# A routed recurrent layer on one core: the slot table emptied group by group, six tiles of ids fetched directly, and five row buffers instead of six

## What is computed

```python
xn = layernorm(x)                              # 4 x 2048 tokens of 512 values
h[t] = h[t-1] * A + xn[t]; s = h @ BC           # recurrence over 8 runs of 1024 tokens
e = argmax(xn @ gate_w.T)                       # one of 8 experts for each token
g = silu(xn + expert_w[e] @ xn)
out = x + s * g
```

## Time and profile before

| | |
|---|---|
| median of 3 runs | 524.4 us (523.9 to 524.87) |
| the profiled execution | 521.92 us |
| its span, first to last instruction | 520.2 us |
| PE busy | 495.5 us, 95% of the span |
| VectorE busy | 409.0 us, 79% |
| ScalarE busy | 260.2 us, 50% |
| POOL busy | 325.1 us, 62% |
| mean granted clock of TensorE | 0.987 |

### The profile page before, as it was taken

How to read it: one execution, slowest core, us unless ns; L and a number is a source line. 1 busy time by engine, 2 the same in 40 slices (tenths; PEclk the granted TensorE clock), 3 DMA queues, 4 the chain that set the end, 5 groups by cost and what they waited for, 6 DMA issues and landing times. The chain is left out here.

```text
span 520.2 us, 10723 instructions
## 1 busy us (share of the span) xinstructions
PE 495.5 (95%) x2739; PEld 389.0 (75%) x2740; DVE 409.0 (79%) x1075; ACT 260.2 (50%) x500; POOL 325.1 (62%) x362
## 2 busy tenths in 40 slices
PE   7959999999999999999996999999999999999993
PEld 6647777777777777777675788888888888887882
DVE  5968998999999998899752777777778777776773
ACT  4647678667767766776621333333333333333330
POOL 3446766676676667667765466666676666656652
PEclk9979999999999999999999999999999999999997
DMA  8996878787788878777336676777767776766620
GB/s 243 394 342 178 258 241 247 233 269 227 253 258 234 249 237 263 228 243 234 120 97 193 224 226 222 234 239 244 249 213 234 235 243 214 232 221 212 222 82 9
DMA packets 65538, 116.99 MB, mean 225 GB/s; under 512 B 8906, under 2 KB 26378, under 8 KB 65428
## 3 DMA queue, kind: packets, MB, share of 16 engines
q1 hardware_dynamic: 47328, 64.59, 39.3%
q0 software_dynamic: 18176, 52.06, 31.6%
HBM read 66.30 MB, written 57.48 MB: 238 GB/s over the span
## 5 line engine op out<-in xcount | busy, mean ns | idle before, releaser
L1073 PE MATMUL ps_s<-w_hi,split 128*128 x284 | 118.2, 416 | 0.2
L643 ACT ACTIVATE ps_s<-ps_s 128x512 f32<-128x512 f32 x71 | 41.3, 582 | 151.4 <-PE ps_s L1075 151.4
L509 POOL DMA_INDIRECT out_dram<-work x71 | 73.7, 1038 | 65.9 <-DVE work L890 52.3
L1074 PE MATMUL ps_s<-w_lo,split 128*128 x284 | 112.4, 396 | 0.0
L1075 PE MATMUL ps_s<-w_hi,split 128*128 x284 | 112.3, 395 | 0.0
L418 POOL TENSOR_TENSOR split<-work,split 128x1024 fp32r<-128x1024 f32 x32 | 77.0, 2406 | 48.4 <-ACT split L571 48.4
L977 PE MATMUL ps_s<-bc_hi,split 128*128 128x512 f32 x256 | 104.6, 409 | 0.5 <-ACT split L571 0.5
L978 PE MATMUL ps_s<-bc_lo,split 128*128 128x512 f32 x256 | 101.5, 396 | 0.0
L436 POOL DMA_INDIRECT slot_table<-token_id,slot_id x64 | 63.0, 985 | 35.2 <-issue 17.3
L499 POOL DMA_INDIRECT work<-token_rows,work x67 | 70.9, 1058 | 21.5 <-issue 19.8
L872 DVE TENSOR_SCALAR work<-work 128x512 f32<-128x512 f32 x71 | 39.3, 554 | 46.1 <-DMA work<-token_rows,work 35.7
(11 more groups left out here) (118 smaller groups left out, 740.1 us busy)
## 6 DMA issues: line engine op xcount, KB each, us to landing
token_rows<-work SPq DMA_DIRECT2D x31, 528.0 KB, 3.2
work<-in_L_attn_inputs_dram SPq DMA_DIRECT2D x31, 512.0 KB, 4.7
token_rows<-work SPq DMA_DIRECT2D x29, 512.0 KB, 5.5
work<-in_L_ffn_expert_w_dram SPq DMA_DIRECT2D x128, 64.0 KB, 3.8
slot_table<-w_lo SPq DMA_DIRECT2D x1, 4160.0 KB, 17.7
token_rows<-in_L_attn_inputs_dram SPq DMA_DIRECT2D x3, 512.0 KB, 13.8
out_dram<-work POOLq DMA_INDIRECT x71, 3.4
work<-token_rows,work POOLq DMA_INDIRECT x67, 4.5
```

What stands on the lines that cost most here:

```text
L509: nc.gpsimd.indirect_dma_start(out=out_flat, out_offset=bass.IndirectOffsetOnAxis(ap=slot_tok[:, n:n + 1], axis=0), in_=o_sb[:, u], in_off ...
L1073: nc.tensor.matmul(z_ps[v], hi, wh, start=(k == 0), stop=False)
L1074: nc.tensor.matmul(z_ps[v], hi, wl, start=False, stop=False)
```

## The change

- The table is emptied in pieces. SP's new `empty(it, c)` writes EMPTY to the two table rows of every expert that group c could need (128 KB), two groups ahead; `scatter_ids` of a group waits for its own piece. `table_end` (64 KB) takes the last 8 rows. The pattern has 128 numbers (512 bytes) in each piece copied, and was 640 numbers. It lies in an SBUF tensor of its own, and no longer in `w_lo`.
- `FIRST` goes from 4 to 6: the ids of six tiles are fetched directly, and the first six `scatter`s use them too.
- `RR`, the number of row buffers, goes from 6 to 5. TensorE's loop keeps its factor of six as `TURN`.
- `all_ids` lands in a place of its own behind the row buffers, and is issued after `gather` of row 3. Its cast and the copy to `slot_tok` move into the loop over tiles, ahead of and behind tile 2.
- In the last groups of stage A, the ranks of the last scores are kept in PSUM, as are those of the first three groups; `high_part` of the last group goes ahead of `take_s` on ScalarE, and `place` of the last but one group goes between the halves of VectorE's scan.

```diff
-    RR = 6
+    RR = 5
-    FILL = 640
+    FILL = 128
+    NEW = GT // P
-    FIRST = 4
+    FIRST = 6
+    TURN = 6
...
+            def empty(it, c):
+                wait(sp, table_empty[c % 2], 16 * rounds(4, it, c, 2))
+                nc.sync.dma_start(table_g[4 * it + c], empty_ids[0:NEW * P * LINE // FILL].unsqueeze(1).to_broadcast(
+                    [NEW * P * LINE // FILL, E, FILL])).then_inc(table_empty[c % 2], 16)
...
             sp.wait_ge(empty_ready, 1)
-            nc.sync.dma_start(table_fill, empty_ids.unsqueeze(1).to_broadcast([P, TROWS * LINE // FILL, FILL])).then_inc(table_empty, 16)
+            for c in range(2):
+                empty(0, c)
+            nc.sync.dma_start(table_end, empty_ids[0:8 * P * LINE // FILL]).then_inc(end_empty, 16)
             for c in range(XR - 1):
                 copy_x(0, c)
             sp.wait_ge(pad_ready, 1)
...
                     load_w(it, c + WR)
+                    empty(it, c + 2)
                     store_s(it, c)
...
                 for v in range(XR):
                     pool.wait_ge(x_stored[v], 16 * (GROUPS // XR - (1 if v < XR - 1 else 0)))
+                wait(pool, o_ready, n - RR + 1)
                 if n < FIRST:
                     pool.wait_ge(ids2_loaded[n], 16)
                     tok = ids2[:, n, 0:1]
                 else:
                     pool.wait_ge(slot_tok_ready, 1)
-                    wait(pool, o_ready, n - RR + 1)
                     tok = slot_tok[:, n:n + 1]
...
-            gather(0, 0)
-            first_ids(2)
+            for c in range(FIRST - 2):
+                gather(0, c)
+                if c < FIRST - 3:
+                    first_ids(c + 2)
             all_ids()
-            gather(0, 1)
-            gather(0, 2)
-            first_ids(3)
-            for c in range(3, RR):
+            first_ids(FIRST - 1)
+            for c in range(FIRST - 2, RR):
                 gather(0, c)
...
             normalise(0, 0)
+            normalise(0, 1)
             low_x2(0, 0)
-            dve.wait_ge(blk_loaded, 16)
-            nc.vector.tensor_copy(blk_f[0:PLANNED], blk_i[0:PLANNED, :, 0]).then_inc(blk_f_ready, 1)
-            normalise(0, 1)
-            dve.wait_ge(slot_turned, 1)
-            nc.vector.tensor_copy(slot_tok[:, :], slot_ps[:, 0:TILES]).then_inc(slot_tok_ready, 1)
+            normalise(0, 2)
             low_x2(0, 1)
-            normalise(0, 2)
             for c in range(TILES):
+                if c == 2:
+                    dve.wait_ge(blk_loaded, 16)
+                    nc.vector.tensor_copy(blk_f[0:PLANNED], blk_i[0:PLANNED, :, 0]).then_inc(blk_f_ready, 1)
                 tile(0, c, ahead=TILES - 1 - c)
+                if c == 2:
+                    dve.wait_ge(slot_turned, 1)
+                    nc.vector.tensor_copy(slot_tok[:, :], slot_ps[:, 0:TILES]).then_inc(slot_tok_ready, 1)
...
-            stay_busy(6)
-            tile(0, 0, ahead=False)
-            turn_x2(0, 1)
-            for c in range(1, RR):
+            stay_busy(4)
+            for c in range(TURN):
                 tile(0, c)
+                if c == 2:
+                    turn_slots()
```

More of the change, by code:

```diff
@@ L49, in bass_recurrent_routed @@
     WR = 2
-    RR = 6
+    RR = 5
     OR = 3
-    LOOPS = TILES // RR - 1
     PAD = 16
@@ L122, in bass_recurrent_routed @@
         slot_tok = part(plan_at, TILES).bitcast(I32)
-        assert plan_at >= at["w"] and plan_at + TILES <= sum(SIZES.values())
-        blk_i = part(FIRST * ROW, P * LINE).bitcast(I32).rearrange("p (q w) -> p q w", w=LINE)
-        assert FIRST * ROW >= 2 * TPG * D
+        assert plan_at >= at["s"] and plan_at + TILES + P * LINE <= sum(SIZES.values())
+        blk_i = part(sum(SIZES.values()) - P * LINE, P * LINE).bitcast(I32).rearrange("p (q w) -> p q w", w=LINE)
+        assert FIRST >= RR
         plan = xnt[:, :, :].rearrange("p c n -> p (c n)")
@@ L145, in bass_recurrent_routed @@
         slot2 = sums(6 + 3 * FIRST, 1)[:, 0:FIRST].bitcast(I32)
[L146 to L148 removed]
+        pick = sums(7 + 3 * FIRST)[:, 0:4]
+        blk_row = sums(7 + 3 * FIRST)[:, 4:5].bitcast(I32)
+        assert sums_at + (8 + 3 * FIRST) * E <= CH * GT and FIRST <= E
+        ids2 = sb("ids2", [P, FIRST, LINE], I32)
         x2_hi = [split[:, v, 0, 0:D] for v in range(2)]
@@ L355, in _ @@
                     load_w(0, c + WR)
+                if c + 2 < GROUPS:
+                    empty(0, c + 2)
                 if c < GROUPS - 1:
@@ L610, in group @@
                     copy_head(it, c + 1)
+                if left == 1:
+                    high_part(0, c + 1)
                 if not start:
@@ L614, in group @@
                     copy_parts(0, 1)
-                if left >= 1:
+                if left >= 2:
                     high_part(it, c + 1)
@@ L673, in variance, with scan @@
                 last.then_inc(var_ready, 1)
-            def scan(it, c):
+            def scan(it, c, between=False):
                 n = U * it + c
@@ L682, in scan @@
                     if k == CH // 2:
+                        if between:
+                            place(it, c - 1, 0)
+                            place(it, c - 1, 1)
                         dve.wait_ge(xnt_tail, n + 1)
@@ L745, in route @@
                 for t in range(TPG):
-                    last = nc.vector.scalar_tensor_tensor(ranked[:, t], points[:, t], top[:, t:t + 1],
+                    last = nc.vector.scalar_tensor_tensor(order[:, t], points[:, t], top[:, t:t + 1],
                                                           prio[:, t], ALU.is_equal, ALU.mult)
@@ L751, in route @@
                 dve.wait_ge(gate_step, 5 * n + 3)
-                nc.vector.tensor_reduce(first[:, :], ranked[:, :, :], AX.X, ALU.max).then_inc(gate_step, 1)
+                nc.vector.tensor_reduce(first[:, :], order[:, :, :], AX.X, ALU.max).then_inc(gate_step, 1)
                 if ahead:
@@ L758, in route @@
                 for t in range(TPG):
-                    last = nc.vector.tensor_scalar(onehot[:, v, t], ranked[:, t], first[:, t:t + 1], None,
+                    last = nc.vector.tensor_scalar(onehot[:, v, t], order[:, t], first[:, t:t + 1], None,
                                                    ALU.is_equal)
@@ L801, in group @@
                 if left >= 1:
-                    scan(it, c + 1)
-                if left == 1:
-                    place(it, c, 0)
-                    place(it, c, 1)
+                    scan(it, c + 1, between=left == 1)
                 if left == 0:
```

48 lines of the change are left out of this document (24 added, 24 removed).

## The result

The changed kernel takes **602.27 us** (median of four runs, 600.80 to 604.91), the kernel before on the same chip 524.15 (four runs, 523.90 to 524.87): a ratio of 1.149 with a 95% interval of 1.145 to 1.154. The forecast was 600 with a range of 590 to 622. The profiled execution is 602.09 us with a span of 599.9; before they were 521.92 and 520.2. On the medians the kernel is 78.1 us slower, and between the two profiled executions the spans differ by 79.7, where the forecast added 75.4.

What follows compares the result with a forecast made beforehand. With five buffers the row buffer's round in stage B, 9.08 us over two tiles, was to set the pace; -6.0 + 3.8 + 84.2 - 4.4 - 2.2 = +75.4 on 524.4 gave 600 us, range 590 to 622.

Steps and rivals of the forecast that it cites:

- start of stage A: Without the single fill ahead of x for group 4, TensorE's scores come at 31.05, not 35.37: 6.0 us removed.
- pieces of the fill: 128 KB for each group of stage A, going into DMA time that is free: taken as 0.
- head of stage B: First tiles of stage B: later id cast and slot_tok put normalise(6) at 299.4, not 295.63: 3.8 us added.
- tiles 6 to 70, empties in them: Stage B: 32 rounds of 9.08 us in place of 206.4 us add 84.2; empty tiles take off 4.4.
- from normalise(70) to the last residual: End of stage B: 9.3 us in place of 11.5, as TensorE has caught up: -2.2.
- L: Stage B: time from a gather's issue to the normalise waiting for its rows, 4.4 us; a round is 4.68 + L.
- The empty tiles: Tiles 68 and 70, taken for empty: gathers land in 2.1 us in place of about 4.4, so -4.4.
- The rule on a GpSimd transfer: Stage B gathers: 2.0 us plus bytes over 436 GB/s, giving 4.2 in place of 4.4; total 6 us shorter.
- The buffer is not missed: Rival: stage B gathers return soon enough, TensorE keeps its pace, 522.2 us; chance 0.05.
- The pieces collide: Rival: the fill's pieces hold up stage A, 618 us or more; chance 0.04.
- The clock: Rival: in stage B TensorE's clock stays at 1.2 GHz and TensorE becomes the bound, 727 us; chance 0.04.
- one gap of 2.6 us: TensorE in each stage B round of 9.08 us: two tiles of 3.24, the other 2.6 us mostly one gap.

Runs made afterwards that it cites:

- pieces_only: The kernel before with the fill of the table in pieces alone, six row buffers: 516.13 us, ratio 0.986; repeated 515.98 us.
- six_early_cast: The changed kernel with six row buffers and the cast and copy of the slot lines around tile 1, not 2: 515.39 us, ratio 0.983; repeated 518.01 us.
- five_only: The kernel before with five row buffers alone, slot lines landing behind them and loaded later: 609.46 us, ratio 1.168.
- four_buffers: The changed kernel with four row buffers instead of five: 894.16 us, ratio 1.71.
- less_matmul: The changed kernel with 8 of the 12 matmuls of a tile: 601.31 us against 602.27.
- vector_order: The changed kernel, five row buffers, with VectorE's turn in the order product, residual, normalise, low_x2: 526.23 us, ratio 1.0056.
- gather_first: The changed kernel, five row buffers, with POOL issuing gather(c + 5) ahead of scatter(c): 565.59 us, ratio 1.079.
- five_best: The changed kernel, five row buffers, with residual first in VectorE's turn, gather ahead of scatter, and the early cast: 523.15 us, ratio 0.998.

## Why the prediction was right

By its own steps, in the profiled execution:

| step | forecast | measured |
|---|---|---|
| start of stage A | -6.0 | -6.7, with the line below |
| pieces of the fill | 0 | 0, by the groups' pace (below) |
| head of stage B | +3.8 | +5.3 |
| tiles 6 to 70, empties in them | +84.2 - 4.4 | +83.4 |
| from normalise(70) to the last residual | -2.2 | -1.7 |
| behind the last residual | 0 | -0.6 |
| sum | +75.4 | +79.7 |

**The start.** The scores were forecast for 31.05:

```profile
29.65 0.83 ACT L566 ACTIVATE work<-work,shift,mv 128x512 f32<-128x512 f32 x1
...
30.80 0.40 PE L961 MATMUL ps_gate<-ident,score_sb 104*128 104x104 f32 x2 [0.85 <-ACT score_sb L582]
...
38.43 0.34 PE L961 MATMUL ps_gate<-ident,score_sb 104*128 104x104 f32 x2
```

They come at 30.80, behind a wait of 0.85 us, and the next at 38.43, a group of 7.63 us instead of 9.31. The first normalise of stage B went from 274.37 to 267.68. `pieces_only` shows the same gain alone, -6.6. That the pieces cost nothing holds too: between 45 and 236 us no engine waits for a DMA, and from the scores at 38.43 to those 27 groups on, at 243.51, are 205.1 us, where 205.3 were (44.68 to 249.94).

**The head.** `slot_tok` was forecast for 293.8 before the 6 us of the start, so for 287.8; it came at 288.84. Timelines of TensorE, then VectorE:

```profile
284.43 0.29 PE L1081 MATMUL ps_gate<-ident,xnt 80*128 80x80 f32 x1 [3.21 <-DVE xnt L925]
285.17 1.09 PE L1075 MATMUL ps_xt<-ident,work 128*128 128x128 f32 x4 [0.45 <-issue]
```

```profile
284.12 0.26 DVE L925 CAST xnt<-work 80x128 f32<-80x128 int32 x1
...
288.84 0.23 DVE L929 CAST work<-ps_gate 128x71 int32<-128x71 f32 x1
...
294.22 0.55 DVE L888 TENSOR_SCALAR work<-work 128x512 f32<-128x512 f32 x1 [5.15 <-DMA work<-token_rows,work]
```

The forecast let TensorE wait some 2.3 us; it waited 3.21, and the four transposes behind it took 1.09 us instead of the 0.60 at full clock. Normalise(6) came at 294.22, where 293.4 was forecast, though stage B had begun 0.7 us sooner than forecast: the term was right in its mechanism and 1.5 us small. Part of this is the clock: the slow transposes made `low_x2` of the next turn wait 0.53 us for ScalarE, and with it the copy to `slot_tok`. With six buffers the early cast takes the loss of the head back (`six_early_cast`: normalise(6) at 289.27, in its repeat 291.22, in `pieces_only` 289.74).

**The rounds.** L was taken as 4.4; the gathers that were waited for took 4.42 on average, from 3.35 to 5.34. The turn was 2.465, the issue 1.33, and residual to scatter 0.89 in the median, where the rows of before had 0.90. From normalise(6) to normalise(66) are 30 rounds: their median is 9.04 us, where 9.08 stood, and their mean 9.16, for which the 4.58 us a tile stand. What lifts the mean is mostly POOL's two late starts, for which the forecast had no term. Residual(19) and its scatter, residual(56) and its scatter:

```profile
368.26 0.69 DVE L906 TENSOR_TENSOR work<-work 128x512 f32<-128x512 f32 x1
371.40 1.03 POOL L525 DMA_INDIRECT out_dram<-work  x1 [4.25 <-issue]
...
537.40 0.69 DVE L906 TENSOR_TENSOR work<-work 128x512 f32<-128x512 f32 x1
541.53 1.02 POOL L525 DMA_INDIRECT out_dram<-work  x1 [4.40 <-issue]
```

They come 2.45 and 3.44 us behind the residual, 1.6 and 2.5 us more than elsewhere, and the rounds there take up to 11.8 us. In all 64 x 0.04 = 2.6 us more than forecast. **The empty tiles** are the other term that was mis-sized, if by little: -4.4 was forecast for two short landings on the chain, but one tile landed in 2.2 us and the other in 3.1, and 64 x 4.58 - 289.7 = 3.4 us were saved. Together the term came out at +83.4 where 79.8 stood, 3.6 of the 4.3 us by which the sum was low. Of the rest, the head was 1.5 us and the way to the last residual 0.5 longer than forecast, the start 0.7 and the end 0.6 shorter. Some luck is in the number: between the profiled executions the forecast was 597.3 us and the time 602.09, while between the medians it was 600 and 602.27, since the median before was 2.5 us above its profiled execution and the changed kernel's only 0.2. The rule on a GpSimd transfer that was weighed in the prediction, the Trainium skill (DMA: Bandwidth & Descriptors, Anatomy of one DMA), with POOL's row of 1.0 an estimate of 4.2 us, would have made the total 6 us lower; the undisturbed landings at 4.31 and 4.30 above lie between it and my 4.4, the mean on the rows' side.

**The rivals.** *The buffer is not missed*: the result, `five_only` and `four_buffers` exclude it. *The pieces collide*: `pieces_only` excludes it. *The clock* is the one that came halfway. The gaps did bring TensorE's clock down, again and again (0.87 in 370 to 410 us, the digits 7 and 8 of the page), and TensorE was busy 528.6 us with the same matmuls that took 495.5 before: the higher busy time is slower work, not more. But the clock came back each time, and `less_matmul` shows that it does not set the pace of the rounds; only in the head did the 0.53 us of above come of it.

**Told wrongly in the list of signs.** TensorE's waits were to be "some 90 us"; its matmul queue waited 51.2 us for the normalise and its weight queue 70.6. The rest of the lost time is in matmuls at the lower clock. And a round's idle time is not always one gap of 2.6 us as I had it: in 13 of 31 rounds the normalises are nearly evenly spaced, some 4.2 and 4.9 us apart, in the others, as in the rows above, some 3.4 and 5.6.

## What to carry to other kernels

A ring of buffers is read as a round: from the instruction that frees a buffer to the transfer, the landing, the consumer, and on to the next freeing instruction behind that consumer. Its length is divided by the number of tiles by which this second freeing instruction is further on. Six, five and four buffers gave 3.24, 4.58 and 9.06 us a tile because that number went from 3 to 2 to 1, and `vector_order` gave 3.37 with five because it made the number 3 again. Before a buffer is given up, move the freeing instruction to the front of its turn: here this was worth 76 us, where the buffer was worth 81. And a large transfer that nobody waits for should still go out in pieces behind those that are waited for: that alone made this kernel 1.4% faster.

## What the runs showed of the hardware

- TensorE's clock fell with waits much shorter than the 5.25 us of before. In the changed kernel its matmul queue waits 1.1 us on average and 3.5 at the longest for a normalise (42 times between 300 and 590 us), and the mean clock is 0.87 to 1.00 by stretches of 40 us. Behind the longest wait the clock is 0.50 (1.2 GHz) from 378 to 383 us. And it fell behind this wait of 1.87 us too, although TensorE had been at work in 10.76 of the 10.8 us before: it is 1.00 from 396 to 397 us and 0.50 from 398 to 400. The 1.86 of before had left it at 1.00, so the length of a single wait does not tell.

```profile
396.66 0.66 PE L1075 MATMUL ps_xt<-ident,work 128*128 128x128 f32 x4 [1.87 <-DVE work L888]
```

- In `four_buffers`, where TensorE waits 3.8 us on average and 5.6 at the longest between 300 and 480 us, the clock is 0.70:

```profile
340.00:380.00 40.00, 26.31 (x78) 19.66 (x79) 11.61 (x20) 5.26 (x9) 9.18 (x9) 0.70 0.24 75
```

- A gather's landing depends little on how busy the DMA engines are once they have room: the gathers that were waited for took 4.31 us on average at a DMA share of 0.24 (`four_buffers`), 4.42 at 0.5 (the changed kernel), 4.48 at 0.60 (`gather_first`), 4.7 in the kernel before with six buffers. Moving other traffic away would shorten this ring's round by 0.1 to 0.4 us at most (an estimate from these means).

- POOL can start a transfer late though nothing that the profile shows holds it: in the changed kernel, `gather_first`, `vector_order`, `less_matmul` and `five_best` by some 1.6 us behind residual(19) and 2.5 us behind residual(56), each time at the same place. The cause is not shown.
